# Expert outputs of a mixture-of-experts decoder: from gathers in the combine step to scatters as each tile is done

## The chip, the cores and the metric

The kernel runs on 1 core of one Trainium2 chip, in one launch. The metric is the time of the whole kernel on the device, in microseconds (us), as the median of several runs. TensorE is called PE here, VectorE DVE, ScalarE ACT, GpSimd POOL and SyncE SP.

## The reference: two decoder layers, each ending in experts

8192 tokens (128 sequences of 64) of 128 numbers pass through six sublayers, and a layer norm without weights stands behind each. Two of them are mixtures of experts: one with two experts for each token, one with a single expert. In short:

```
x = norm(x + self_attention(x))
x = norm(x + cross_attention(x, ctx))
x = norm(x + moe2(x))        # 8 experts, top 2, softmax of the two scores as gates
x = norm(x + memory(x))      # a recurrence over 64 steps
x = norm(x + gelu_mixer(x, ctx))
x = norm(x + moe1(x))        # 8 experts, top 1, its probability as gate

moe2: scores = x @ Wg.T; top 2; gates = softmax(the two scores)
      y_e = (silu(x @ W1[e].T) * (x @ W2[e].T)) @ W3[e].T
      out = sum over the two experts of gate * y_e
moe1: probs = softmax(x @ Wr + br); gate, e = max, argmax
      out = gate * (relu(x @ W1[e] + b1[e]) @ W2[e] + b2[e])
```

## The kernel before, in words

**Stages.** Each stage is a block of its own, in which five engine programs run beside each other and wait for each other by counting semaphores; all engines meet between blocks. In the order of time: self attention, cross attention, the top-2 experts (`run_experts`, called "the first expert stage" below, its tiles named `ffn_run_*`), the memory (products, recurrence), the mixer, and the top-1 experts ("the second expert stage", same names). The 8192 tokens are 64 tiles of 128 tokens; tile number t of the tokens lies in `x_all[:, t, :]` in SBUF.

**Routing.** `route` on DVE works out, for one half of the token tiles at a time (`HALF` = 32), at which row of a table sorted by expert each token stands (`dest`). POOL then scatters the tokens' rows into that table in DRAM (`tokens_by_expert`, one indirect DMA of 128 rows for each tile and choice). Each half has its own part of the table, with places left empty so that each 128 rows belong to one expert. The first half's scatters (64 in the first expert stage, 32 in the second) are issued on POOL in the last part of the stage before. `route` for the second half is the last work of that stage, so the second half's scatters are issued inside `run_experts`.

**The expert tiles.** `run_experts` goes over 144 (top 2) or 80 (top 1) tiles of 128 rows of the sorted table; `MID` is half of that. SP loads four tiles at a time. For tile i PE transposes it (L1135), ACT copies the transposed tile (L1168) and the weights of its expert (L1169), PE multiplies (L1143), ACT and DVE make the hidden values (L1176 and L1242 for top 2; L1248 and L1181 for top 1), PE multiplies again (L1152), and DVE copies the result out of PSUM (L1258, or L1260 with a bias). `y_copied` counts these copies. Every four tiles SP stores them to `expert_outputs` in DRAM (L1066), in the order of the sorted table. The first half of the loop is a loop in the code; from `MID` on DVE, SP and POOL have it written out.

**The combine.** A group g is four token tiles, so there are 16 groups. POOL gathers, for each token tile and choice, the 128 rows of `expert_outputs` that belong to its tokens (L1115, 8 indirect DMAs for a group in the first expert stage, 4 in the second). DVE multiplies by the gate and adds the residual (L1200), takes the statistics (L1211, L1216, L1221), POOL takes the power -0.5 (`root`, L1099), DVE normalises (L1228) and SP stores (L1059). The first 8 groups need only the first `MID` expert tiles and run beside the second half of the loop; the last 8 need all tiles and run behind the loop. On POOL's queue stand, in this order: the second half's scatters, each held back until `y_copied` has come within five tiles of it (`turn > 4`), then for each group its gathers and, behind the gathers of group g, `root(g - 1)`.

**The empty rows.** The sorted table is filled with zeros once, in self attention: SP issues two DMAs of 64 KB for each of the 64 tiles (L369) and 16 more behind its loop (L401).

Of the kernel before, what the change touches and what calls it, by code (L numbers as in the profile page):

```python
# [15 lines left out]
P = 128  # L16
# [6 lines left out]
LN_EPS = 1e-5  # L23

# [211 lines left out]
def zeros_for(nc, mk, xs):  # L236

    zeros = mk.sb("zeros", [P, D])
    zeros_set, filled = mk.sem("zeros_set"), mk.sem("xs_filled")
    with nc.Block() as block:  # L240

        @block.vector
        def _(dve):
            dve.memset(zeros[:, :], 0.0).then_inc(zeros_set, 1)
    return {"zeros": zeros, "set": zeros_set, "filled": filled, "xs": [half.rearrange("(n p) d -> n p d", p=P) for half in xs]}


def attention(nc, stage, k, x_in, ctx_in, mask_in, w, x_out, fill=None, f=None, xs=None):
# [3 lines left out]
    with ExitStack() as ctx:  # L252
# [91 lines left out]
        def _(sp):  # L344
# [20 lines left out]
            def step(i):  # L365
                t = i
                if t.exists() and fill:
                    for half in fill["xs"]:
                        sp.dma_start(half[t.n], fill["zeros"][:, :]).then_inc(fill["filled"], 16)  # L369
# [9 lines left out]
                if t.exists():  # L379
                    sp.wait_ge(y_normed, t.count())  # L380
                    dst = f.x_all[:, bass.ds(t.n, 1), :].rearrange("p a d -> p (a d)") if f else out_v[t.n]
                    sp.dma_start(dst, y[:, t.slot(Y), :]).then_inc(stored[t.slot(Y)], 16)
# [15 lines left out]
            if fill:  # L398
                for n in range(NT, Sorted2.ALL // 2):
                    for half in fill["xs"]:  # L400
                        sp.dma_start(half[n], fill["zeros"][:, :]).then_inc(fill["filled"], 16)  # L401
            for n in range(Y):
                sp.wait_ge(stored[n], 16 * NT // Y)

        @block.gpsimd
        def _(pool):
# [36 lines left out]
            else:  # L443
                f.tables(pool)

                def late(i):
                    step(i)
                    if i.c == middle:
# [3 lines left out]
                        pool.wait_ge(f.filled, 16 * Sorted2.ALL)  # L452
                    if i.c < middle + HALF:
                        f.scatter(pool, xs, i.c - middle)
                half_way(pool, step, 4, 4, Tile, middle, late=late, peeled=8)
                for t in range(NT + 4 - middle, HALF):
                    f.scatter(pool, xs, t)
# [344 lines left out]
class Experts:  # L802


    def __init__(self, nc, ctx, stage, a, top2, scattered, gathered):
# [16 lines left out]
        self.x_all = sb("x_all", [P, NT, D])  # L822
        self.dest = sb("dest", [P, K, NT], U32)
        self.source = sb("source", [P, K, NT], U32)
# [20 lines left out]
        self.source_f = sb("source_f", [P, K, HALF])  # L845
# [8 lines left out]
        self.scattered, self.gathered = scattered, gathered  # L854
# [5 lines left out]
    def tables(self, pool):  # L860
# [9 lines left out]
        pool.wait_ge(self.made, 5)  # L870
# [3 lines left out]
    def count_tokens(self, pe, counts, h):  # L874

        pe.wait_ge(self.made, 6)
# [12 lines left out]
    def scatter(self, pool, xs, t):  # L889

        for r in range(self.K):
            self.scatter_one(pool, xs, t, r)

    def scatter_one(self, pool, xs, t, r):

        pool.indirect_dma_start(xs[t // HALF], bass.IndirectOffsetOnAxis(ap=self.dest[:, r, t:t + 1], axis=0), self.x_all[:, t, :], None)\  # L896
            .then_inc(self.scattered, 16)

    def route(self, dve, counts, h):
# [23 lines left out]
        dve.wait_ge(self.made, 6)  # L923
# [49 lines left out]
        link(ts(self.source_f[:, :, :], self.dest_f[:, :, :], float(h * (T // 2 * P)), None, ALU.add))  # L973
        dve.tensor_copy(self.source[:, :, mine], self.source_f[:, :, :])
# [6 lines left out]
        if self.top2:  # L981
# [3 lines left out]
            link(tt(self.gate[:, 1, mine], small["e2"][:, :], self.gate[:, 0, mine], ALU.mult))  # L985


def run_experts(nc, f, k, xs, ys, x_out):
# [3 lines left out]
    MID = kind.ALL // 2  # L992
    w_up, w_down, b_up, b_down, expert_of, x_all, gate = f.w_up, f.w_down, f.b_up, f.b_down, f.expert_of, f.x_all, f.gate
# [21 lines left out]
    with ExitStack() as ctx:  # L1015
        mk = Maker(nc, ctx, stage + "_run")
        sb, ps, sem = mk.sb, mk.ps, mk.sem
        x = sb("x", [P, 2, 4, D])
        y = sb("y", [P, 2, 4, D])
# [6 lines left out]
        r1 = sb("r1", [P, 4, D])  # L1026
        r = sb("r", [P, 2, 4, D])
        stats = sb("stats", [P, 2, 4, 6])
        mv = sb("mv", [P, 2, 4, 2])
        ve = sb("ve", [P, 2, 4])  # L1030
        rstd = sb("rstd", [P, 2, 4])
# [1098 lines left out]
```

## Time and profile before

| What | Value |
|---|---|
| Time of the kernel, median of 3 runs | 2066.25 us (2063.7 to 2067.76) |
| Span of the profiled execution, first to last instruction | 2131.4 us |
| First expert stage: first to last copy out of PSUM | 794.8 to 1060.3 us of the span |
| From there to the next stage's first DMA | 1060.6 to 1168.3 us |
| Second expert stage: first to last copy out of PSUM | 1882.7 to 2065.1 us |
| From there to the end | 2065.4 to 2131.4 us |
| PE, DVE, ACT, POOL busy over the span | 64%, 66%, 52%, 47% |

The profiled execution has no time of its own beside its span: the span is what the trace gives, and it is 65 us longer than the median of the runs without a profile. All durations below are from the profiled execution.

### The profile page before, as it was taken

The numbers are of one execution on the slowest core, as the hardware profiler recorded it, in microseconds if no ns is written. First come the engines' busy times: TensorE is split into PE (matmuls) and PEld (weight loads), VectorE is DVE, ScalarE is ACT, GpSimd is POOL, SyncE is SP. The second block draws the span as 40 slices with busy tenths as digits, with TensorE's granted clock in tenths as the row PEclk, the third lists the DMA queues.
The fourth block names the chain that finished last, engine by engine and source line by source line (L and its number), as shares of the span: only waits on it lengthen the run. The fifth ranks groups of instructions, "written<-read, shape, count | busy, mean of one in ns | idle before, by whom it ended". The sixth has DMA issues, their size and how long they took to land. (4 is left out here: it accounts for less than half of the span.)

```text
span 2131.4 us, 61164 instructions
## 1 busy us (share of the span) xinstructions
PE 1357.8 (64%) x18328; PEld 1105.5 (52%) x18383; DVE 1406.7 (66%) x4922; ACT 1101.9 (52%) x3264; POOL 994.8 (47%) x1543
## 2 busy tenths in 40 slices
PE   6999984799978738788700899400001786679850
PEld 4777762677756527787700577300000665479750
DVE  4999982688776643346634566499997677644565
ACT  4777762577746525555500455365555565456430
POOL 3666661455558855435475344111112455842345
PEclk9999995999989959999955899755555998889985
DMA  1222221311112113334322244300000422222232
GB/s 39 76 74 74 74 65 47 102 50 54 45 47 68 58 49 104 102 91 123 109 64 58 69 100 100 53 1 1 1 1 16 144 74 64 71 84 78 78 88 70
DMA packets 218918, 141.81 MB, mean 67 GB/s; under 512 B 22380, under 2 KB 207254, under 8 KB 218646
## 3 DMA queue, kind: packets, MB, share of 16 engines
q1 hardware_dynamic: 206486, 114.94, 20.1%
q0 software_dynamic: 12288, 25.19, 3.8%
q8 instruction: 61, 1.00, 0.2%
q14 instruction: 83, 0.68, 0.1%
HBM read 75.92 MB, written 55.67 MB: 62 GB/s over the span
## 5 line engine op out<-in xcount | busy, mean ns | idle before, releaser
L1143 PE MATMUL ffn_run_up_ps<-ffn_run_xt,ffn_run_w_now 128*128 128x128 f32 x1792 | 251.5, 285 | 72.0 <-ACT ffn_run_w_now L1169 39.2
L1143 PEld LDWEIGHTS ffn_run_up_ps<-ffn_run_xt,ffn_run_w_now 128*128 128x128 f32 x1792 | 225.5, 197 | 87.1 <-ACT ffn_run_xt L1168 59.3
L896 POOL DMA_INDIRECT tokens_by_expert<-ffn_x_all,ffn_dest x192 | 192.1, 1001 | 137.6 <-DVE ffn_run_y L1258 47.2
L1115 POOL DMA_INDIRECT ffn_run_yg<-expert_outputs,ffn_source x192 | 185.0, 963 | 142.0 <-issue 59.7
L1862 PE MATMUL mixer_m_ps<-mixer_mine,mem_state_coef 128*64 128x64 f32 x4 | 0.5, 334 | 283.7 <-DVE mixer_off_in L2003 283.7
L1152 PE MATMUL ffn_run_y_ps<-ffn_weights,ffn_run_h 128*128 x1216 | 175.2, 278 | 0.8 <-DVE ffn_run_y L1258 0.4
L1152 PEld LDWEIGHTS ffn_run_y_ps<-ffn_weights,ffn_run_h 128*128 128x128 f32 x1216 | 156.8, 195 | 1.1 <-issue 1.1
L1242 DVE TENSOR_TENSOR ffn_run_h<-ffn_run_up_ps,ffn_run_act 128x256 f32<-128x256 f32 x144 | 60.6, 421 | 144.0 <-ACT ffn_run_act L1176 121.1
L1588 POOL TENSOR_TENSOR recur_rho<-recur_var_eps_new,k_half 128x1 f32<-128x1 f32 x64 | 34.7, 543 | 248.1 <-DVE recur_var_eps_new L1682 248.1
L1862 PEld LDWEIGHTS mixer_m_ps<-mixer_mine,mem_state_coef 128*64 128x64 f32 x4 | 0.3, 204 | 283.8 <-DVE mixer_ones L2001 283.8
L1169 ACT COPY ffn_run_w_now<-ffn_weights 128x512 f32 x224 | 140.3, 626 | 0.0
L429 POOL TENSOR_TENSOR self_k_ex<-self_kt,k_head_mask 128x256 f32<-128x256 f32 x128 | 75.8, 613 | 120.0 <-ACT self_kt L646 120.0
L429 POOL TENSOR_TENSOR cross_k_ex<-cross_kt,k_head_mask 128x256 f32<-128x256 f32 x128 | 75.9, 614 | 110.4 <-ACT cross_kt L646 110.0
L1841 POOL TENSOR_TENSOR mixer_rstd<-mixer_ve,k_half 128x1 f32<-128x1 f32 x128 | 69.1, 553 | 84.0 <-DVE mixer_ve L2029 83.7
L1168 ACT COPY ffn_run_xt<-ffn_run_xt_ps 128x128 f32<-128x128 f32 x224 | 58.4, 261 | 92.8 <-PE ffn_run_xt_ps L1135 67.4
L714 DVE TENSOR_REDUCE cross_top<-cross_s_ps_ps 128x16 f32<-128x1024 f32 x64 | 77.9, 1217 | 26.4 <-PE cross_s_ps_ps L519 19.1
L1248 DVE TENSOR_TENSOR ffn_run_sums<-ffn_run_up_ps,ffn_weights 128x512 f32<-128x512 f32 x80 | 55.1, 688 | 58.9 <-PE ffn_run_up_ps L1143 37.3
L1200 DVE SCALAR_TENSOR_TENSOR ffn_run_r<-ffn_run_yg,ffn_gate,ffn_x_all 128x128 f32<-128x128 f32 x128 | 43.6, 340 | 76.0 <-DMA ffn_run_yg<-expert_outputs,ffn_source 72.9
L1176 ACT ACTIVATE ffn_run_act<-ffn_run_up_ps 128x256 f32<-128x256 f32 x144 | 55.5, 386 | 72.2 <-PE ffn_run_up_ps L1143 61.4
L714 DVE TENSOR_REDUCE self_top<-self_s_ps_ps 128x16 f32<-128x1024 f32 x64 | 77.8, 1215 | 14.7 <-PE self_s_ps_ps L523 14.7
L1181 ACT ACTIVATE ffn_run_h<-ffn_run_sums 128x512 f32<-128x512 f32 x80 | 50.4, 630 | 70.0 <-DVE ffn_run_sums L1248 65.6
L1135 PE MATMUL ffn_run_xt_ps<-k_ident,ffn_run_x 128*128 128x128 f32 x224 | 62.3, 280 | 33.9 <-DMA ffn_run_x<-tokens_by_expert 33.9
(367 smaller groups left out, 4830.2 us busy)
## 6 DMA issues: line engine op xcount, KB each, us to landing
ffn_run_x<-tokens_by_expert SPq DMA_DIRECT2D x56, 256.0 KB
expert_outputs<-ffn_run_y SPq DMA_DIRECT2D x56, 256.0 KB
tokens_by_expert<-fill_zeros SPq DMA_DIRECT2D x144, 64.0 KB, 1.6
memory_rows<-products_row SPq DMA_DIRECT2D x16, 390.0 KB, 4.7
ffn_weights<-memory_rows SPq DMA_DIRECT2D x16, 390.0 KB
self_x<-in_x SPq DMA_DIRECT2D x64, 64.0 KB, 1.9
self_xr<-in_x SPq DMA_DIRECT2D x64, 64.0 KB, 1.9
x<-self_y SPq DMA_DIRECT2D x64, 64.0 KB, 1.5
```

Of the source, the lines that this page charges most:

```text
L429: pool.tensor_tensor(k_ex[:, t.slot(2), b, :, :], kt[:, t.slot(2), b * S:(b + 1) * S].unsqueeze(1).to_broadcast([P, 4, S]), k["head_mask4" ...
L714: dve.tensor_reduce(top[:, t.slot(2), :].rearrange("p (q h) -> p q h", q=4), s_ps, AX, ALU.max).then_inc(top_ready, 1)
L896: pool.indirect_dma_start(xs[t // HALF], bass.IndirectOffsetOnAxis(ap=self.dest[:, r, t:t + 1], axis=0), self.x_all[:, t, :], None)\
L1115: pool.indirect_dma_start(yg[:, g % 4, n, m, :], None, rows, bass.IndirectOffsetOnAxis(ap=f.source[:, m, 4 * g + n:4 * g + n + 1], axis=0))\
L1135: nc.tensor.transpose(xt_ps[t.slot(2)][:, 0:P], x[:, slot, t.c % 4, :], k["ident"][:, :]).then_inc(x_turned, 1)
L1143: mm = nc.tensor.matmul(up_ps[t.slot(2)][:, c * P:(c + 1) * P], w_now[:, t.slot(2), c * P:(c + 1) * P], xt[:, t.slot(2), :], start=True, s ...
L1152: mm = nc.tensor.matmul(y_ps[t.slot(2)][:, 0:D], h[:, t.slot(4), c, :], w_down[:, bass.ds(e_now, 1), c, :], start=(c == 0), stop=(c == FC ...
L1168: act.copy(xt[:, t.slot(2), :], xt_ps[t.slot(2)][:, 0:P]).then_inc(x_copied, 1)
L1169: act.copy(w_now[:, t.slot(2), :], w_up[:, bass.ds(e_ahead, 1), :].rearrange("p a n -> p (a n)")).then_inc(w_taken, 1)
L1176: act.activation(act1[:, t.slot(2), :], up_ps[t.slot(2)][:, 0:HID], ACT.Silu).then_inc(silu_ready, 1)
L1242: dve.tensor_tensor(h[:, t.slot(4), :, :].rearrange("p c n -> p (c n)"), up_ps[s2][:, HID:2 * HID], act1[:, s2, :], ALU.mult)\
L1841: pool.tensor_tensor(rstd[n][:, s2, :], ve[n][:, s2, :], k["half"][:, 0:1], ALU.pow).then_inc(rstd_ready[n], 1)
```

## The change

Each row of the sorted table is now 130 numbers wide: the token's 128, the number of the row its result is to go to (1 + 2 * token + choice, or 1 + token), and, for top 2, its gate. `x_all` has the two extra columns. POOL sets the row number with an iota, adds one before the second choice is scattered (`relabelled`), and copies the gates of the choice into place. Scatters go choice by choice, no longer tile by tile, and are no longer held back by `y_copied`. DVE reads number and gate back from each loaded tile (`ids`, `gates`; a row that was left empty has the number 0 and is sent to a spare row of its own), multiplies by the gate as it copies the result out of PSUM, and puts the result into `y_all`, which holds all tiles. POOL scatters each tile from there to `expert_outputs`, which is now in the order of the tokens. The combine reads four token tiles with one plain DMA on SP (`fetch`). DVE adds (two additions of 128x512 for a group for top 2, four multiply-and-adds for top 1) and works out `shift` = -mean * rstd; the normalisation is ACT's (`norm`, an activation with scale and bias). Groups 0 to 7 are combined two for every eight tiles from tile `START` on (96 of 144, or 48 of 80). Groups have four buffers where they had two. ACT's second half of the loop is now written out too. The zero fill is 64 larger DMAs for four tables (the second expert stage has its own now), none behind the loop.

```diff
-    def scatter_one(self, pool, xs, t, r):
-        pool.indirect_dma_start(xs[t // HALF], bass.IndirectOffsetOnAxis(ap=self.dest[:, r, t:t + 1], axis=0), self.x_all[:, t, :], None)\
-            .then_inc(self.scattered, 16)
+    def scatter(self, pool, xs, h, n):
+        r, t = n // HALF, h * HALF + n % HALF
+        mine = slice(h * HALF, (h + 1) * HALF)
+        if n == HALF:
+            pool.wait_ge(self.scattered[h], 16 * HALF)
+            pool.tensor_scalar(self.x_all[:, mine, D], self.x_all[:, mine, D], 1.0, None, ALU.add).then_inc(self.relabelled, 1)
+        if self.top2 and n % HALF == 0:
+            pool.wait_ge(self.gated, h + 1)
+            pool.tensor_copy(self.x_all[:, mine, D + 1], self.gate[:, r, mine]).then_inc(self.relabelled, 1)
+            pool.wait_ge(self.relabelled, 3 * h + 1 + 2 * r)
+        pool.indirect_dma_start(xs[h], bass.IndirectOffsetOnAxis(ap=self.dest[:, r, t:t + 1], axis=0), self.x_all[:, t, :], None)\
+            .then_inc(self.scattered[h], 16)
...
         @block.gpsimd
         def _(pool):
-            for t in range(HALF, NT):
-                for m in range(K):
-                    turn = K * (t - HALF) + m
-                    if turn > 4:
-                        pool.wait_ge(y_copied, turn - 4)
-                    f.scatter_one(pool, xs, t, m)
...
-                for n in range(4):
-                    for m in range(K):
-                        turn = K * (4 * g + n) + m
-                        if g < N_G // 2 and turn > 3:
-                            pool.wait_ge(y_copied, MID + turn - 3)
-                        pool.indirect_dma_start(yg[:, g % 4, n, m, :], None, rows,
...
+            for n in range(K * HALF):
+                f.scatter(pool, xs, 1, n)
+            for t in range(kind.ALL):
+                pool.wait_ge(y_copied, t + 1)
+                pool.indirect_dma_start(ys, bass.IndirectOffsetOnAxis(ap=ids[:, t:t + 1], axis=0), y_all[:, t, :], None)\
+                    .then_inc(stored[t // MID], 16)
+                u, part = (t - START) // 8, (t - START) % 8
+                if t >= START and part == 5 and u < 4:
+                    root(2 * u)
+                    root(2 * u + 1)
+            for g in range(N_G // 2, N_G):
+                root(g)
...
         @block.sync
         def _(sp):
+            def fetch(g):
+                if g >= 4:
+                    sp.wait_ge(summed, g - 3)
+                sp.dma_start(yg[:, g % 4, :, :, :], ys_v[g]).then_inc(fetched[g % 4], 16)
...
-                if t.exists() and t.c % 4 == 3:
-                    n, slot, uses = four(t)
-                    sp.wait_ge(y_copied, t.count())
-                    sp.dma_start(ys_v[n], y[:, slot, :, :]).then_inc(stored[slot], 16)
...
+                    if part == 0 and u == 0:
+                        sp.wait_ge(stored[0], 16 * MID)
+                    if part == 0 and u < 4:
+                        fetch(2 * u)
+                        fetch(2 * u + 1)
...
         @block.scalar
+                for n in tiles:
+                    no = act.activation(out[:, s4, n, :], r[:, s4, n, :], ACT.Identity, bias=shift[:, s4, n:n + 1], scale=rstd[:, s4, n:n + 1])
...
         @block.vector
+                if top2:
+                    dve.tensor_tensor(r1[:, :, :], yg[:, s4, :, 0, :], x_all[:, mine, 0:D], ALU.add).then_inc(partly, 1)
+                    dve.wait_ge(partly, g + 1)
+                    dve.tensor_tensor(r[:, s4, :, :], yg[:, s4, :, 1, :], r1[:, :, :], ALU.add).then_inc(summed, 1)
...
-                        dve.tensor_copy(y[:, slot, t.c % 4, :], y_ps[t.slot(2)][:, 0:D]).then_inc(y_copied, 1)
+                        dve.tensor_scalar(mine, y_ps[t.slot(2)][:, 0:D], gates[:, slot, t.c % 4:t.c % 4 + 1], None, ALU.mult).then_inc(y_copied, 1)
...
+                if i.static and START <= i.c < kind.ALL:
+                    u, part = (i.c - START) // 8, (i.c - START) % 8
+                    if u < 4 and part in (0, 2):
+                        add(2 * u + part // 2)
+                    elif u < 4 and part in (1, 3):
+                        spread(2 * u + part // 2)
+                    elif u < 4 and part == 4:
+                        moments(2 * u)
+                        moments(2 * u + 1)
+                    if 1 <= u < 5 and part == 3:
+                        shifts(2 * u - 2)
+                        shifts(2 * u - 1)
```

POOL's queue in the first expert stage, before: the 64 scatters of the second half, the gathers (`ffn_run_yg`) of groups 0 and 1, and then 8 gathers and a `root` (`ffn_run_rstd`) in turn.

```order
L896 DMA tokens_by_expert<-ffn_x_all,ffn_dest 9216x128 x64
L1115 DMA ffn_run_yg<-expert_outputs,ffn_source 128x128 x16
L1099 TENSOR_TENSOR ffn_run_rstd<-ffn_run_ve,k_half 128x4
L1115 DMA ffn_run_yg<-expert_outputs,ffn_source 128x128 x8
L1099 TENSOR_TENSOR ffn_run_rstd<-ffn_run_ve,k_half 128x4
```

The same queue of the changed kernel, from the start of the stage.

```order
L1125 IOTA ffn_run_spare 128x144
L1127 TENSOR_SCALAR ffn_run_spare<-ffn_run_spare 128x144
L903 COPY ffn_x_all<-ffn_gate 128x32
L905 DMA tokens_by_expert<-ffn_x_all,ffn_dest 9216x130 x32
L900 TENSOR_SCALAR ffn_x_all<-ffn_x_all 128x32
L903 COPY ffn_x_all<-ffn_gate 128x32
L905 DMA tokens_by_expert<-ffn_x_all,ffn_dest 9216x130 x32
L1132 DMA expert_outputs<-ffn_run_y_all,ffn_run_ids 34817x128 x102
L1123 TENSOR_TENSOR ffn_run_rstd<-ffn_run_ve,k_half 128x4 x2
L1132 DMA expert_outputs<-ffn_run_y_all,ffn_run_ids 34817x128 x8
```

No gather is left; 144 scatters of results stand behind the 64 of tokens, and the first two roots stand behind the scatter of tile 101.

DVE's program in the first expert stage, before, where a group is combined beside the loop: two steps of the loop, each with a quarter of group 0.

```order
L1242 TENSOR_TENSOR ffn_run_h<-ffn_run_up_ps,ffn_run_act 128x256
L1258 COPY ffn_run_y<-ffn_run_y_ps 128x128
L1200 SCALAR_TENSOR_TENSOR ffn_run_r<-ffn_run_yg,ffn_gate,ffn_x_all 128x128
L1200 SCALAR_TENSOR_TENSOR ffn_run_r<-ffn_run_yg,ffn_gate,ffn_run_r 128x128
L1211 BN_STATS ffn_run_stats<-ffn_run_r 128x6
```

The changed kernel, steps 98 to 100 of the loop (the second group of a pair, then the moments of both).

```order
L1290 TENSOR_TENSOR ffn_run_h<-ffn_run_up_ps,ffn_run_act 128x256
L1307 TENSOR_SCALAR ffn_run_y_all<-ffn_run_y_ps,ffn_run_gates 128x128
L1235 TENSOR_TENSOR ffn_run_r<-ffn_run_yg,ffn_x_all 128x512
L1237 TENSOR_TENSOR ffn_run_r<-ffn_run_yg,ffn_run_r 128x512
L1290 TENSOR_TENSOR ffn_run_h<-ffn_run_up_ps,ffn_run_act 128x256
L1307 TENSOR_SCALAR ffn_run_y_all<-ffn_run_y_ps,ffn_run_gates 128x128
L1251 BN_STATS ffn_run_stats<-ffn_run_r 128x6 x4
L1290 TENSOR_TENSOR ffn_run_h<-ffn_run_up_ps,ffn_run_act 128x256
L1307 TENSOR_SCALAR ffn_run_y_all<-ffn_run_y_ps,ffn_run_gates 128x128
L1258 BN_AGGR ffn_run_mv<-ffn_run_stats 128x2 x4
L1263 TENSOR_SCALAR ffn_run_ve<-ffn_run_mv 128x4
```

A quarter of a group for each step has become the whole addition in one step, the whole statistics in the next, and the moments of two groups in a third; the normalisation is gone from DVE.

## Rows read from the trace of the kernel before

**Rows 1.** Busy time by stage: stretch, length, then each engine's busy us.
```profile
783.60:1061.00 277.40, 227.42 (x1872) 216.29 (x1872) 128.66 (x456) 158.87 (x433) 131.43 (x136) 0.97 0.36 104
1061.00:1168.20 107.20, 0.00 (x0) 0.00 (x0) 42.85 (x169) 0.00 (x0) 70.19 (x72) 0.51 0.23 64
1872.00:2065.40 193.40, 163.65 (x1360) 158.82 (x1360) 102.80 (x293) 104.90 (x240) 69.80 (x72) 0.96 0.29 83
2065.40:2131.40 66.00, 0.00 (x0) 0.00 (x0) 32.33 (x140) 0.00 (x0) 39.38 (x40) 0.51 0.26 76
```

**Rows 2.** POOL's groups behind the first loop: count, busy us, mean ns, idle.
```profile
L1115 POOL DMA_INDIRECT ffn_run_yg<-expert_outputs,ffn_source x64 | 61.8, 966 | 22.8 <-issue 22.8
L1099 POOL TENSOR_TENSOR ffn_run_rstd<-ffn_run_ve,k_half 128x4 f32<-128x4 f32 x8 | 8.4, 1050 | 8.6 <-DVE ffn_run_ve L1221 8.5
```

**Rows 3.** Timeline, both ends of the two stretches behind the loops.
```profile
1060.33 0.29 DVE L1258 COPY ffn_run_y<-ffn_run_y_ps 128x128 f32<-128x128 f32 x1
...
1161.25 1.62 SPq L1059 DMA_DIRECT2D x<-ffn_run_out  x2
...
2065.05 0.29 DVE L1260 TENSOR_TENSOR ffn_run_y<-ffn_run_y_ps,ffn_weights 128x128 f32<-128x128 f32 x1 [0.20 <-PE ffn_run_y_ps L1152]
...
2113.72 0.95 POOL L1115 DMA_INDIRECT ffn_run_yg<-expert_outputs,ffn_source  x1 [0.30 <-issue]
...
2116.27 0.35 DVE L1200 SCALAR_TENSOR_TENSOR ffn_run_r<-ffn_run_yg,ffn_gate,ffn_x_all 128x128 f32<-128x128 f32 x1 [1.76 <-DMA ffn_run_yg<-expert_outputs,ffn_source]
...
2120.48 1.62 SPq L1059 DMA_DIRECT2D decoded<-ffn_run_out  x2
```

**Rows 4.** Copies out of PSUM by stretch: length, DVE busy (count).
```profile
794.50:906.50 112.00, 16.55 (x59) 1.00 0.33 99
908.50:928.50 20.00, 3.65 (x13) 1.00 0.36 100
973.00:1060.70 87.70, 14.05 (x50) 1.00 0.41 114
...
1984.00:2065.40 81.40, 9.03 (x32) 0.94 0.30 84
```

**Rows 5.** DVE's groups, 973 to 1061 us.
```profile
L1242 DVE TENSOR_TENSOR ffn_run_h<-ffn_run_up_ps,ffn_run_act 128x256 f32<-128x256 f32 x48 | 20.0, 417 | 22.2 <-ACT ffn_run_act L1176 13.9 <-issue 6.5 <-PE ffn_run_y_ps L1152 1.8
```

**Rows 6.** DVE's groups, 1984 to 2065.4 us.
```profile
L1248 DVE TENSOR_TENSOR ffn_run_sums<-ffn_run_up_ps,ffn_weights 128x512 f32<-128x512 f32 x30 | 20.5, 683 | 3.6 <-PE ffn_run_up_ps L1143 3.5
L1200 DVE SCALAR_TENSOR_TENSOR ffn_run_r<-ffn_run_yg,ffn_gate,ffn_x_all 128x128 f32<-128x128 f32 x32 | 10.9, 339 | 10.8 <-DMA ffn_run_yg<-expert_outputs,ffn_source 10.8
L1211 DVE BATCH_NORM_STATS2 ffn_run_stats<-ffn_run_r 128x6 f32<-128x128 f32 x32 | 9.4, 295 | 1.1
L1260 DVE TENSOR_TENSOR ffn_run_y<-ffn_run_y_ps,ffn_weights 128x128 f32<-128x128 f32 x32 | 9.0, 282 | 1.4 <-PE ffn_run_y_ps L1152 1.4
L1228 DVE TENSOR_SCALAR ffn_run_out<-ffn_run_r,ffn_run_mv,ffn_run_rstd 128x128 f32<-128x128 f32 x29 | 8.6, 363 | 10.4 <-POOL ffn_run_rstd L1099 10.4
L1216 DVE BATCH_NORM_AGGREGATE ffn_run_mv<-ffn_run_stats 128x2 f32<-128x6 f32 x32 | 3.0, 156 | 0.0
L1221 DVE TENSOR_SCALAR ffn_run_ve<-ffn_run_mv 128x4 f32<-128x4 f32 x8 | 1.4, 170 | 0.3
```

**Rows 7.** POOL's timeline, start of the first expert stage.
```profile
784.33 0.97 POOL L896 DMA_INDIRECT tokens_by_expert<-ffn_x_all,ffn_dest  x1 [12.06 <-POOLq L154]
785.60 0.97 POOL L896 DMA_INDIRECT tokens_by_expert<-ffn_x_all,ffn_dest  x1 [0.30 <-issue]
```

**Rows 8.** DMAs by line: KB of one, median us from issue to landing.
```profile
products_x<-x SPq DMA_DIRECT2D x16, 256.0 KB, 3.0
ffn_weights<-in_L_ffn_b SPq DMA_DIRECT2D x1, 512.0 KB, 5.0
```

**Rows 9.** An ACT activation with a bias for each partition: min/median/max ns.
```profile
L649 ACT ACTIVATE cross_qt<-cross_front_ps,cross_b_cols x64: 358/359/380, 353.5 to 726.5; 128x128 f32<-128x128 f32 x64
```

**Rows 10.** SP's timeline, end of self attention.
```profile
321.35 7.55 SPq L401 DMA_DIRECT2D tokens_by_expert<-fill_zeros  x16
332.68 0.34 SPq L347 DMA_DIRECT2D cross_w_t<-in_L_xattn_Wq  x1
```

More of the change, by code:

```diff
@@ L802, with __init__ @@
 class Experts:
-    def __init__(self, nc, ctx, stage, a, top2, scattered, gathered):
+    def __init__(self, nc, ctx, stage, a, top2, scattered, stored):
         self.nc, self.stage, self.a, self.top2 = nc, stage, a, top2
@@ L874, in count_tokens @@
     def count_tokens(self, pe, counts, h):
-        pe.wait_ge(self.made, 6)
+        pe.wait_ge(self.made, 7)
         pe.wait_ge(self.selected, h + 1)
@@ L1076, in _ @@
-            sp.wait_ge(f.scattered, 16 * K * HALF)
-            half_way(sp, step, 8, 1, kind, MID - 8, second)
-            for g in range(PER * (MID // 8 - 2), N_G):
+                if i.static and i.c >= START - 4:
+                    u, part = (i.c - START + 4) // 8, (i.c - START + 4) % 8
+                    if part == 0 and u == 0:
[3 more added lines that the diff above has]
+                        fetch(2 * u + 1)
+                    if part == 6 and u >= 2:
+                        keep(2 * u - 4)
+                        keep(2 * u - 3)
@@ new lines, in _ @@
+            sp.wait_ge(f.scattered[0], 16 * K * HALF)
+            half_way(sp, step, 8, 0, kind, MID - 8, second)
+            sp.wait_ge(stored[1], 16 * MID)
+            first = [2 * u - 4 + n for u in range(2, 6) if START - 4 + 8 * u + 6 >= kind.ALL for n in range(2)]
+            for g in range(N_G // 2, N_G):
+                fetch(g)
+                if first:
+                    keep(first.pop(0))
+                if g >= N_G // 2 + 3:
+                    keep(g - 3)
+            for g in range(N_G - 3, N_G):
@@ L1122, in _ @@
+            for g in range(N_G // 2, N_G):
+                root(g)
         @block.tensor
@@ L1266, in _ @@
+            dve.wait_ge(numbered, 2)
             half_way(dve, step, 3, 0, kind, MID)
+            if START + 32 + 3 >= kind.ALL:
+                shifts(N_G // 2 - 2)
+                shifts(N_G // 2 - 1)
             for g in range(N_G // 2, N_G):
-                for part in range(5):
-                    combine(g, part, 4 * (g + 1))
+                add(g)
+                spread(g)
+                moments(g)
                 if g > N_G // 2:
-                    combine(g - 1, 6)
-                    combine(g - 1, 7)
```

284 lines of the change are left out of this document (145 added, 139 removed).

## The prediction, made before the changed kernel had run

> **What bounds the kernel now.** I read the busy time by stage first. In the two stretches behind the expert loops, 107.2 and 66.0 us long, PE and ACT do nothing at all and DVE is busy less than half the time; POOL is busy for 70.2 and 39.4 us [rows 1]. The groups of POOL say with what: 64 gathers of 966 ns each and 8 roots [rows 2]. Two indirect DMAs that wait for nothing start 1.27 us apart [rows 7], so 64 of them take 81 us whatever the data. The timeline gives the length to be compared: from the last copy out of PSUM (1060.33) to the end of the last store's issue (1162.87) 102.5 us, and in the second stage from 2065.05 to 2122.10, 57.0 us [rows 3]. These two stretches are bound by POOL's issue of gathers.
>
> Inside the loops I counted copies by stretch. In the first stage they come every 1.90 us while POOL scatters tokens (59 in 112 us), every 1.54 us where no indirect DMA runs (13 in 20 us), and every 1.75 us beside the combine (50 in 87.7 us) [rows 4]. So PE could go at 1.54, and something in the company of POOL's DMAs costs up to 0.36 us for each tile. In the second stage the combine's half takes 2.54 us for a tile (32 in 81.4 us) [rows 4], and DVE's groups there show why: 10.8 us of waiting for gathered rows and 10.4 us for roots, which stand behind gathers on POOL [rows 6].
>
> **The change part by part.**
>
> *Behind the first loop.* No gather is left. After the last copy (0.29 us) comes one scatter, whose rows can be used 2.55 us after its issue if I take the last gather's case (2113.72 to 2116.27) [rows 3]; no row shows the landing of a scatter. Then a fetch of 512 KB, 5.0 us by a load of the same size [rows 8]. Together 7.8 us. The eight groups are then DVE's: two additions of 128x512 at 0.683 (the same form from PSUM), four statistics at 0.295, four aggregates at 0.156, and two small operations at 0.170 [rows 6] make 3.5 us, with waits for its own results 3.6; eight groups 28.8 us. Behind the last group one root, 1.05 us [rows 2], the shift, four normalisations at 0.36 us [rows 9], hops and the store's issue: 3.5 us. Sum 40.1 instead of 102.5: **62 us less**. The transfers should hide: 512 KB read for a group at 5.0 us alone is more than DVE's 3.6, but four fetches are issued ahead. Were they not to overlap at all, eight would take 40 us and the gain would be 51.
>
> *Behind the second loop.* A fetch of 256 KB is 3.0 us [rows 8]: 5.8 us to the first group. A group is four multiply-and-adds at 0.339 and the rest as above, 3.5 us; eight are 28, and 3.5 behind. Sum 37.3 instead of 57.0: **20 us less**.
>
> *The second loop.* For eight tiles with two groups DVE has 8 x (0.683 + 0.282) = 7.7, adds 2.7, statistics 2.4, aggregates 1.2, four small operations 0.7, the row numbers 0.7, and some ten waits for its own results, 1.5: 17 us or 2.1 for a tile [rows 6]. The normalisation's 0.363 us for each of 32 tiles [rows 6] is ACT's now. Over 32 tiles 67 us instead of 81.4: **14 us less**. POOL isn't late here: 32 token scatters are 41 us, and 1.27 for a tile is less than 2.1.
>
> *The first loop.* POOL has 64 + 144 scatters of 1.27 us. It starts at 784.3 [rows 7]; 1.2 us for the row numbers, 81.3 for 64 scatters, and 2.6 for the drain before the second choice is relabelled: 869.4. Scatter of tile t ends at 869.4 + 1.27 (t + 1), so POOL is about 40 tiles behind and gains on the loop. Tile 101 is done at 999, the two roots behind it at 1001. DVE waits for them in step 107. Tile 96 is copied at about 977 now; from there eight tiles with two groups are 8 x (0.417 + 0.34) for the two operations of a tile [rows 5], 2.7 for additions, 2.4 + 1.2 + 0.7, row numbers and gates 1.0, own waits 1.8: 15.9 us, 2.0 a tile. Step 107 comes at 999: the roots are just late, by 2 us. SP's wait for the first 72 results (869.4 + 91.4 + 2.6 = 963) lies before its step at 970 and holds nothing; behind it are the next loads of tiles. ACT's two normalisations in four steps of eight add 0.36 each, which fits in 2.0. End of the loop: 977 + 32 x 2.0 + 16 x 1.75 = 1069, with the wait 1071, where it is 1060 now: **11 us more**.
>
> *The same loop without a profile.* The span is 65 us above the median of the runs. If part of that is the 0.36 us a tile in the first 60 tiles, the loop before is up to 22 us shorter in the runs that are timed, but the changed one isn't, since POOL's 1001 us doesn't move: DVE and PE just wait for it. Bounds 0 and 25 us; I take the middle, since nothing in the trace says how much: **12 us more**.
>
> *The rest.* The 16 fills behind self attention's loop take 7.55 us of SP, and the next stage begins 3.8 us after them [rows 10]; the last stores need some 1.5 us of that anyway, and a block that clears semaphores is new: **4.5 us less**. Fills inside the loop shrink from two DMAs a tile to one, SP having room. In cross attention POOL's relabelling comes some 3 us after the scatter it waits for, so it costs only its own two small operations; with those, a longer memset and more semaphores to clear I put **1.5 us more**. Wider rows (520 bytes for 512) have no row; I take them as equal, and up to 2 us a stage as the other end.
>
> *Sum:* 62 + 20 + 14 + 4.5 - 11 - 12 - 1.5 = 76 us of the span, from 2131 to 2055. The runs stand to the span as 2066 to 2131, so 74 us off the median: **1993 us**.
>
> **A rule against it.** Through the stretch behind the first loop POOL's indirect DMAs run beside DVE's operations between SBUF buffers and keep a mean of 966 ns [rows 2], against 970 ns for the first two of the stage with DVE idle [rows 7]. The Trainium skill, page "SBUF — State Buffer", section "SBUF: two separate sides", says that while DVE runs a two-port operation GpSimd is locked out and cannot write its descriptors. By that rule every scatter would be later by an operation's length; by the trace it adds nothing.
>
> **Rivals.**
> 1. *Scatters of results cost more than those of tokens* (slower). With a price c for each of 208 scatters the first stage's POOL ends at 784 + 13 + 208 c. At c = 1.27 that is 1061, inside the loop. Each scatter that waited for one DVE operation of 0.34 us would make c 1.61 and POOL's end 1132: 61 us lost, gain 13 of the span, about 2053. The gain is gone at c = 1.68; at 1.9 POOL ends at 1192 and the kernel takes about 2110. That is the mechanism of the page's rule. Against it: 966 and 970 ns. Chance 8% for slower, 2% within 0.2%.
> 2. *The combine in lumps holds the loops back.* One step takes two additions of 128x512, the next four statistics, a third both groups' moments, and ACT's two normalisations follow. PE's buffers allow about two tiles of slack. If these steps don't average out, 2.5 us a tile for the 32 tiles of each stage: 16 + 13 us more, about 2021; with serial fetches behind the loop 2031. For it: own waits in each lump. Chance 16%.
> 3. *The loops lose their other stalls too.* SP's stores of four tiles are gone, and DVE doesn't wait for gathers in the loop. If the first loop ends as it does now (1060) and nothing of the 12 us comes, 23 us better: about 1971. POOL's end at 1061 allows no more. Chance 14%.
> 4. *My forecast*, 60%, with its own range 1975 to 2012.
>
> **How the numbers follow.** Range: down to rival 3 with some room, 1958; up to rival 2 with serial fetches, 2033. Faster by over 0.2% (4 us, about what a measurement of this kernel can tell from no change): 0.90, same 0.02, slower 0.08.
>
> **What the changed profile would show.** Behind the loops: no POOL DMA but the last, DVE busy with few gaps, 40 and 37 us to the last store. POOL in the first stage: 208 indirect DMAs 1.27 us apart to about tile 110, then waiting for copies. Copies every 1.9 us up to tile 96, then 2.0; a wait of DVE for a root near 1000 us. The forecast is wrong if POOL's pitch isn't 1.27, if copies with the combine come at 2.5 us, if fetches leave DVE idle between groups, or if the loop's pace in the first 72 tiles changes.

## The result, and the profile after

The changed kernel takes **2002.16 us** (median of 4 runs, 2000.04 to 2004.25) where the kernel before takes 2066.89: a ratio of 0.9688, 95% interval 0.9674 to 0.9701, or 65 us less. The forecast was 1993 us with a range of 1958 to 2033.

The trace that stands ahead of the prediction is of an execution 65 us longer than the timed runs. So the kernel before was run again (b_again, below): that execution has a span of 2063.6 us, the changed kernel's has 1998.3, and these two are compared here.

Busy time by stage, first of the kernel before in b_again (stretch, length, busy us of PE, weight loads, DVE, ACT and POOL, then granted clock, DMA share, GB/s). The rows are cross attention, the first loop, what is behind it, memory and mixer, the second loop, what is behind it.

```profile
331.20:769.00 437.80, 325.29 (x6393) 255.22 (x6393) 300.62 (x623) 247.06 (x656) 257.04 (x390) 0.90 0.20 58
769.00:1000.40 231.40, 219.47 (x1872) 212.00 (x1872) 126.90 (x455) 165.48 (x433) 131.74 (x136) 0.98 0.43 125
1000.40:1105.20 104.80, 0.00 (x0) 0.00 (x0) 43.40 (x170) 0.00 (x0) 69.95 (x72) 0.51 0.24 65
1105.20:1809.30 704.10, 346.07 (x2668) 251.70 (x2668) 533.01 (x2723) 369.22 (x1418) 234.46 (x488) 0.75 0.21 53
1809.30:1997.60 188.30, 164.61 (x1360) 160.23 (x1360) 103.10 (x293) 104.89 (x240) 69.78 (x72) 0.94 0.30 86
1997.60:2063.60 66.00, 0.00 (x0) 0.00 (x0) 32.33 (x140) 0.00 (x0) 39.35 (x40) 0.51 0.27 76
```

The same of the changed kernel:

```profile
326.60:764.50 437.90, 327.01 (x6393) 255.68 (x6393) 299.86 (x619) 246.77 (x656) 258.62 (x395) 0.90 0.20 58
764.50:1038.40 273.90, 227.00 (x1872) 217.37 (x1872) 129.87 (x492) 176.12 (x465) 209.67 (x219) 0.92 0.36 108
1038.40:1080.50 42.10, 0.00 (x0) 0.00 (x0) 22.72 (x96) 13.07 (x32) 11.76 (x10) 0.52 0.51 155
1080.50:1787.30 706.80, 348.31 (x2668) 253.40 (x2668) 531.08 (x2719) 370.11 (x1418) 235.78 (x490) 0.75 0.22 53
1787.30:1955.50 168.20, 159.50 (x1360) 155.25 (x1360) 100.25 (x310) 114.01 (x263) 115.08 (x119) 0.97 0.33 94
1955.50:1998.30 42.80, 0.00 (x0) 0.00 (x0) 20.90 (x114) 16.67 (x42) 11.90 (x12) 0.53 0.44 126
```

Row by row the 65.3 us between the two spans come apart, with 331.2 less 326.6 for self attention:

| Stretch | Forecast | Measured |
|---|---|---|
| Self attention and its boundary | -4.5 | -4.6 |
| Cross attention | +1.5 | +0.1 |
| First loop | +23 (11 and 12) | **+42.5** |
| Behind the first loop | -62 | -62.7 |
| Memory and mixer | 0 | +2.7 |
| Second loop | -14 | -20.1 |
| Behind the second loop | -20 | -23.2 |
| Sum | -76 | -65.3 |

The +2.7 of memory and mixer wasn't traced to a cause. The first loop is the row to look at. It was PE's: busy for 219.5 of 231.4 us. Now it is 42.5 us longer with the same matmuls, while POOL's busy time went from 131.7 to 209.7. POOL's groups in it (count, busy us, mean ns, idle before and its releasers):

```profile
L1132 POOL DMA_INDIRECT expert_outputs<-ffn_run_y_all,ffn_run_ids x144 | 140.1, 973 | 43.7 <-issue 33.8 <-DVE ffn_run_y_all L1307 9.9
L905 POOL DMA_INDIRECT tokens_by_expert<-ffn_x_all,ffn_dest x64 | 61.5, 961 | 19.5 <-issue 18.9 <-POOL ffn_x_all L903 0.6
L1123 POOL TENSOR_TENSOR ffn_run_rstd<-ffn_run_ve,k_half 128x4 f32<-128x4 f32 x8 | 8.5, 1068 | 0.1
```

Busy and idle of these three rows are 273.4 us; with 3 us for row numbers and gates that is all of the time from the stage's start (764.5) to the end of the last scatter (1040.8). 208 indirect DMAs take 264.8 of it, 1.27 us each, and none of the result scatters waited for a copy longer than 0.5 us. What DVE does meanwhile, in its timeline (start, duration, operation, idle time before and its releaser):

```profile
924.59 0.34 DVE L1307 TENSOR_SCALAR ffn_run_y_all<-ffn_run_y_ps,ffn_run_gates 128x128 f32<-128x128 f32 x1
944.83 0.69 DVE L1235 TENSOR_TENSOR ffn_run_r<-ffn_run_yg,ffn_x_all 128x512 f32<-128x512 f32 x1 [19.89 <-DMA ffn_run_yg<-expert_outputs]
...
979.56 0.16 DVE L1269 SCALAR_TENSOR_TENSOR ffn_run_shift<-ffn_run_mv,ffn_run_rstd 128x4 f32<-128x4 f32 x1 [13.75 <-POOL ffn_run_rstd L1123]
```

DVE reaches tile 96 at 924.6 and waits 19.9 us for the first fetch, which waits for POOL's scatter of tile 71 (it ends at 939.4, SP issues the fetch at 940.7); then 13.7 us for the first root, which stands behind the scatter of tile 101. Both waits are for POOL.

Behind the first loop, where [rows 3] had 102.5 us between the last copy and the end of the last store's issue:

```profile
1039.84 0.96 POOL L1132 DMA_INDIRECT expert_outputs<-ffn_run_y_all,ffn_run_ids  x1 [0.30 <-issue]
...
1046.08 0.69 DVE L1235 TENSOR_TENSOR ffn_run_r<-ffn_run_yg,ffn_x_all 128x512 f32<-128x512 f32 x1 [7.68 <-DMA ffn_run_yg<-expert_outputs]
...
1048.98 0.69 DVE L1235 TENSOR_TENSOR ffn_run_r<-ffn_run_yg,ffn_x_all 128x512 f32<-128x512 f32 x1
...
1065.80 7.96 SPq L1082 DMA_DIRECT2D x<-ffn_run_out  x4
```

The last scatter can be used 2.2 us after its issue (SP's fetches start at 1042.08), the first group's rows are there at 1046.08, and a group takes 2.90 us from one addition to the next. From the last copy (1038.05) to 1073.76 it is 35.7 us.

### The profile page after: what moved, and what is told of

The parts are those of the page before. It is cut to its first block and busy times, and to the rows that moved or that the text cites. A ratio compares the mean times of both kernels' runs of the same rounds, so it can differ in the third digit from the quotient of the medians.

```text
span 1998.3 us, 61159 instructions
## 1 busy us (share of the span) xinstructions
PE 1350.8 (68%) x18382; PEld 1097.1 (55%) x18383; DVE 1371.0 (69%) x4870; ACT 1158.3 (58%) x3392; POOL 1034.6 (52%) x1587
## 5 line engine op out<-in xcount | busy, mean ns | idle before, releaser
L1162 PE MATMUL ffn_run_up_ps<-ffn_run_xt,ffn_run_w_now 128*128 128x128 f32 x1792 | 249.8, 284 | 47.6 <-DVE ffn_run_h L1290 20.3
L1132 POOL DMA_INDIRECT expert_outputs<-ffn_run_y_all,ffn_run_ids x224 | 218.4, 975 | 87.5 <-issue 46.4
L718 DVE TENSOR_REDUCE self_top<-self_s_ps_ps 128x16 f32<-128x1024 f32 x64 | 77.7, 1214 | 14.7 <-PE self_s_ps_ps L527 14.7
L1187 ACT ACTIVATE ffn_run_out<-ffn_run_r,ffn_run_shift,ffn_run_rstd 128x128 f32<-128x128 f32 x128 | 53.4, 483 | 57.6 <-DVE ffn_run_shift L1269 57.6
L1447 POOL TENSOR_TENSOR products_rr<-products_mse,k_half 128x1 f32<-128x1 f32 x64 | 34.6, 541 | 95.8 <-DVE products_mse L1600 87.4
L644 ACT COPY self_prob_t<-self_pt_ps_ps 128x512 f32<-128x512 f32 x128 | 68.9, 589 | 20.7 <-PE self_pt_ps_ps L562 20.7
```

What stands on the lines that cost most here:

```text
L644: act.copy(prob_t[:, 4 * h:4 * h + 4, :], pt_ps[h][:, :, :]).then_inc(pt_copied, 1)
L718: dve.tensor_reduce(top[:, t.slot(2), :].rearrange("p (q h) -> p q h", q=4), s_ps, AX, ALU.max).then_inc(top_ready, 1)
L1132: pool.indirect_dma_start(ys, bass.IndirectOffsetOnAxis(ap=ids[:, t:t + 1], axis=0), y_all[:, t, :], None)\
L1162: mm = nc.tensor.matmul(up_ps[t.slot(2)][:, c * P:(c + 1) * P], w_now[:, t.slot(2), c * P:(c + 1) * P], xt[:, t.slot(2), :], start=True, s ...
```

## Experiments

Every ratio is to the kernel before, in the runs of the same chip; the changed kernel's is 0.9688.

**b_again: the kernel before, once more, with a profile.**

> The kernel before, unchanged, for a second profile. If its span was long because of the recording itself, the span is near 2131 us again and copies of the first stage come every 1.9 us. If that one execution was disturbed, the span is near 2066 us, and the 65 us are missing in places that can be read: I look at the first stage's copies (1.9 or 1.55 us a tile), cross attention (435 or 423 us) and the two stretches behind the loops.

It took 2065.44 us (one run), its trace spans 2063.6. Copies out of PSUM by stretch (length, DVE busy and count, clock, DMA share, GB/s), of b_again and then of the changed kernel:

```profile
779.50:891.50 112.00, 20.16 (x72) 1.00 0.38 115
```

```profile
775.30:887.30 112.00, 24.63 (x72) 1.00 0.33 95
```

72 copies in 112 us in both, where [rows 4] had 59. The pace of 1.90 us was that execution's and not the kernel's; so was the 1.75 us beside the combine (b_again has the last 72 copies in 109.0 us, 1.51 each), and so was 13 us of cross attention (450.9 there, 437.8 here), and in all the first loop was 45.6 us longer there (277.0 for 231.4, by the same cut). What slowed that one execution isn't shown: the single operations took as long there as in b_again (a matmul of L1143 279 and 278 ns), the gaps between them were longer.

**b_nohold: the wait of token scatters left out.**

```diff
-                    if turn > 4:
-                        pool.wait_ge(y_copied, turn - 4)
```

> The kernel before without the wait that holds each token scatter back until the copies have come within five tiles. Theory A, POOL's indirect DMAs in company slow the loop by 0.36 us a tile: the 64 scatters are over after 81 us, some 45 tiles, and 15 tiles go faster, 5 us less in all. Theory B, the wait itself slows the loop (POOL waking on each copy): copies come every 1.55 us from the first tile on, about 20 us less. Theory C, neither does, and the pace of 1.9 was that execution's: no change within 4 us.

2066.4 us, ratio 0.9999 (0.9984 to 1.0015). That is theory C: the 5 us of theory A and the 20 of theory B lie outside the interval, so neither POOL's DMAs in company nor the hold slow the loop by such amounts.

**b_nohold2: the wait of the first eight groups' gathers left out.**

```diff
-                        if g < N_G // 2 and turn > 3:
-                            pool.wait_ge(y_copied, MID + turn - 3)
```

> The kernel before without the wait that holds the gathers of the first eight groups back to one for each copy. In the second stage's combine half DVE waited 10.5 us for gathered rows and 10.4 us for roots. If this hold is what makes the rows late, both go and the kernel is about 20 us faster. If the rows are late because gathers stand on POOL's queue behind a root that waits up to 14.7 us for DVE's variance, nothing changes (within 3 us).

Ratio 1.001 (0.9995 to 1.0025): the hold costs nothing. What does cost time is seen on POOL's timeline in b_again's second stage:

```profile
1911.02 0.94 POOL L1115 DMA_INDIRECT ffn_run_yg<-expert_outputs,ffn_source  x1 [0.30 <-issue]
1926.68 1.05 POOL L1099 TENSOR_TENSOR ffn_run_rstd<-ffn_run_ve,k_half 128x4 f32<-128x4 f32 x1 [14.71 <-DVE ffn_run_ve L1221]
1927.92 1.00 POOL L1115 DMA_INDIRECT ffn_run_yg<-expert_outputs,ffn_source  x1 [0.19 <-issue]
```

The next gathers stand behind a root that waits 14.7 us for DVE, and DVE then waits for them, 10.5 us in all by its groups there, and 10.4 us for roots:

```profile
L1200 DVE SCALAR_TENSOR_TENSOR ffn_run_r<-ffn_run_yg,ffn_gate,ffn_x_all 128x128 f32<-128x128 f32 x32 | 10.9, 339 | 10.5 <-DMA ffn_run_yg<-expert_outputs,ffn_source 10.5
...
L1228 DVE TENSOR_SCALAR ffn_run_out<-ffn_run_r,ffn_run_mv,ffn_run_rstd 128x128 f32<-128x128 f32 x30 | 8.8, 362 | 10.4 <-POOL ffn_run_rstd L1099 10.4
```

In the changed kernel's second loop DVE waits for neither in that half, only for PE. 20.9 us of waits went, the loop is 20.1 us shorter. That the one makes the other is read from the two traces; no run took these waits out alone.

**a_extra: more scatters for POOL.**

```diff
+                if t < (24 if top2 else 12):
+                    pool.indirect_dma_start(other, bass.IndirectOffsetOnAxis(ap=ids[:, t:t + 1], axis=0), y_all[:, t, :], None)\
+                        .then_inc(stored[0], 16)
```

> The changed kernel with more work for POOL: the results of the first 24 tiles of the first expert stage, and of the first 12 of the second, are scattered a second time, into a table that nothing reads. In the changed kernel's trace POOL issues in the first stage without a pause to 1040.8 us; in the second it waits for copies. If POOL's issue bounds the first stage, it ends 24 x 1.27 = 30 us later and the second stays as it is (12 x 1.27 = 15 us fit in its waits): 30 us slower, about 2032 us. If the first stage were bound by its loop's lumps and POOL only kept up, less than 10 us slower. If POOL bounds the second too, 45.

2037.53 us, ratio 0.9867 (0.9837 to 0.9897). The two loops of its trace:

```profile
767.40:1071.90 304.50, 229.18 (x1872) 219.54 (x1872) 130.56 (x492) 176.26 (x465) 233.01 (x243) 0.87 0.34 102
...
1819.80:1993.70 173.90, 161.08 (x1360) 156.44 (x1360) 100.39 (x310) 114.01 (x263) 126.40 (x131) 0.96 0.33 96
```

The first is 30.6 us longer for 24 scatters, 1.27 each: POOL's issue is the first loop's length. The second, where I expected nothing, is 5.7 longer: with 15 us more POOL is late there too, for the fetches at the start of its combine, for which DVE waits 4.3 us. So the span is 36.5 us longer than the changed kernel's (2034.8 for 1998.3) and not 30.

**a_start108: the first stage's combine from tile 108.**

```diff
-    START = MID + (24 if top2 else 8)
+    START = MID + (36 if top2 else 8)
```

> The changed kernel with the combine of the first stage started at tile 108 instead of 96. There DVE waited 19.9 us for the first fetch and 13.7 us for the first root. If POOL's 208 indirect DMAs and 8 roots bound the stage (they fill it from its start to 1040.8 us), both waits cost nothing: the same time within 3 us. If the waits cost what they last, 20 to 30 us faster.

2001.35 us, ratio 0.9692 (0.9673 to 0.9711): the same. Its loop and what is behind it:

```profile
762.50:1033.30 270.80, 227.01 (x1872) 215.96 (x1872) 130.28 (x491) 173.00 (x457) 207.16 (x218) 0.93 0.36 107
1033.30:1078.00 44.70, 0.00 (x0) 0.00 (x0) 22.80 (x99) 16.25 (x40) 13.63 (x12) 0.54 0.52 159
```

DVE's waits didn't go, they moved: 3.8 us for fetches and 29.7 for roots in the loop, 33.5 together, where the changed kernel has 20.3 and 14.6, 34.9 together. They are where DVE sits out what POOL is late by, at whatever place it meets POOL. POOL's last scatter ends 275.1 us behind the stage's start (1037.6 less 762.5) where it was 276.3; the last copy comes 3.1 us earlier, and the stretch behind it is 2.6 longer.

**a_pair: one root for two groups.**

```diff
+            def roots(u):
...
+                pool.tensor_tensor(rstd[:, s4:s4 + 2, :], ve[:, s4:s4 + 2, :], k["half"][:, :].unsqueeze(1).to_broadcast([P, 2, 4]), ALU.pow)\
+                    .then_inc(rstd_ready, 2)
```

> The changed kernel with one root for the two groups of a pair (four POOL operations on 128x8 instead of eight on 128x4 beside the loop, in each expert stage). If POOL bounds the first stage, each root left out takes 1.0 us off its end: 4 us faster, none of it in the second stage. If the loop's own pace bounds it, no change.

2001.97 us, ratio 0.9686 (0.9664 to 0.9708). The form of the expectation held, its size didn't: a root on 128x8 takes 1.67 us, two on 128x4 2.08, so four pairs save 1.6 us and not 4, too little for these runs to show.

```profile
L1130 POOL TENSOR_TENSOR ffn_run_rstd<-ffn_run_ve,k_half x8: 1667/1674/2014, 980.3 to 1956.9; 128x8 f32<-128x8 f32 x8
```

**a_dvenorm: the normalisation on DVE.**

```diff
-                    no = act.activation(out[:, s4, n, :], r[:, s4, n, :], ACT.Identity, bias=shift[:, s4, n:n + 1], scale=rstd[:, s4, n:n + 1])
+                    no = dve.tensor_scalar(out[:, s4, n, :], r[:, s4, n, :], rstd[:, s4, n:n + 1], shift[:, s4, n:n + 1], ALU.mult, ALU.add)
```

> The changed kernel with the normalisation on DVE again (one operation with scale and shift for each token tile, as it stands in ACT's program now, at the same places). By my account DVE has 0.36 us more for each of 128 tiles. Behind each loop DVE is what the time is made of: 8 x 1.45 = 11.6 us more in each, 23 in all. In the first loop POOL bounds and nothing is added. In the second, DVE has 17 us of waiting for PE in 85 us: if that takes it up, nothing more, 2025 us in all; if lumps can't be taken up, up to 11.6 more, 2037 us. If ACT's part had been worth nothing, no change.

2009.43 us, ratio 0.973 (0.970 to 0.976). Its four stretches:

```profile
764.30:1036.00 271.70, 226.86 (x1872) 217.68 (x1872) 137.92 (x524) 166.26 (x433) 208.12 (x218) 0.91 0.37 108
1036.00:1085.60 49.60, 0.00 (x0) 0.00 (x0) 31.26 (x129) 0.00 (x0) 11.33 (x11) 0.52 0.45 132
1790.80:1958.00 167.20, 157.81 (x1360) 154.26 (x1360) 105.12 (x333) 105.42 (x240) 115.36 (x119) 0.98 0.33 95
1958.00:2007.80 49.80, 0.00 (x0) 0.00 (x0) 32.34 (x156) 0.00 (x0) 11.38 (x12) 0.51 0.38 108
```

No loop is longer (271.7 for 273.9, 167.2 for 168.2), each stretch behind one is 7 us longer (49.6 for 42.1, 49.8 for 42.8). ACT's part is worth some 7 us behind each loop and nothing in them. I had 11.6 for each and so 2025 us in all: four such operations in a row take 1.12 us and not 4 x 0.36, which makes 9.0; the rest of the difference isn't traced.

**a_pooladd: an addition of each group behind the first loop on POOL.**

```diff
+            def first_add(g):
+                pool.wait_ge(fetched[g % 4], (g // 4 + 1) * 16)
+                pool.wait_ge(summed, g - 1)
+                pool.tensor_tensor(r1[:, g % 2, :, :], yg[:, g % 4, :, 0, :], x_all[:, 4 * g:4 * g + 4, 0:D], ALU.add).then_inc(partly, 1)
```

> The changed kernel with the first of the two additions of 128x512 of each group behind the first loop given to POOL, which only has a root for each group there. A group is 2.92 us of DVE now, 0.72 of it this addition. If POOL's addition (some 1.2 us by its 128x256 multiplication of 0.61) runs beside DVE at no cost to it, 8 x 0.72 = 5.8 us less: 1996 us. If operations of POOL and DVE between SBUF buffers hold each other up, the gain is gone, or it is some microseconds slower.

2002.2 us, ratio 0.9693 (0.9665 to 0.9722): nothing. The profiled execution was the slowest of the four (2010.62 us, the others 2001.0 to 2002.4), so its lengths are not compared, only what waited for what. The first two groups came 2.2 us apart. Later DVE waited twice, 3.0 and 2.8 us, for an addition of POOL that itself waited for a fetch:

```profile
1063.17 1.18 POOL L1141 TENSOR_TENSOR ffn_run_r<-ffn_run_yg,ffn_x_all 128x512 f32<-128x512 f32 x1 [2.44 <-DMA ffn_run_yg<-expert_outputs]
...
1064.48 0.69 DVE L1248 TENSOR_TENSOR ffn_run_r<-ffn_run_yg,ffn_run_r 128x512 f32<-128x512 f32 x1 [3.04 <-POOL ffn_run_r L1141]
```

SP's queue shows why the fetches were late:

```profile
1058.55 0.38 SPq L1082 DMA_DIRECT2D x<-ffn_run_out  x1
1058.97 0.51 SPq L1078 DMA_DIRECT2D ffn_run_yg<-expert_outputs  x1
1060.89 0.38 SPq L1082 DMA_DIRECT2D x<-ffn_run_out  x1
1061.31 0.51 SPq L1078 DMA_DIRECT2D ffn_run_yg<-expert_outputs  x1
```

Each fetch stands behind the store of a group four earlier, whose normalisation it doesn't need.

**a_fetch** puts these fetches two groups ahead; **a_best** adds POOL's addition and the start at tile 108.

```diff
-                if g >= N_G // 2 + 3:
-                    keep(g - 3)
-            for g in range(N_G - 3, N_G):
+                if g >= N_G // 2 + 5:
+                    keep(g - 5)
+            for g in range(N_G - 5, N_G):
```

> The changed kernel with another order on SP behind the loops: the fetches of groups 12 to 15 stand two groups ahead of where they stood, no longer behind the store of a group whose buffer they don't need. In the changed kernel DVE waited only 0.2 us for those fetches, so alone this is worth nothing: the same within 3 us.

> Together: the first addition of each group behind the first loop on POOL, the earlier fetches, and the combine of the first stage from tile 108 on. With POOL's addition alone the groups came 2.2 to 2.9 us apart until DVE and POOL waited for fetches that stood behind stores on SP. If that order was what ate the gain, groups come every 2.3 us, 8 x 0.65 = 5 us less behind the loop, and up to 3 us less in the loop: 1994 us. If the transfers themselves (512 KB of fetch and 256 KB of store for each group) are the limit at some 2.9 us a group, nothing is gained behind the loop, and it takes 1999 to 2002 us.

1998.13 us, ratio 0.9671 (0.9656 to 0.9686), and 1999.33 us, 0.9674 (0.9659 to 0.969). The first isn't told from the changed kernel (the intervals overlap; the stretch behind its first loop is 41.5 us for 42.1). In the second the groups came 2.2 and 2.9 us apart in turn, 2.5 on average and not 2.3, and from the third group on neither DVE nor POOL waited for a fetch. So neither the order on SP nor the transfers set that pace. The last section shows what lengthens every second group.

**a_again and a_pf: the changed kernel, and the version without the later start.**

> The changed kernel, unchanged, on the same chip as the next one, to compare the two directly: 2002 us if the runs so far are typical of it, within 3 us.

> The changed kernel with POOL's addition and the earlier fetches, and with the combine from tile 96 on as in the changed kernel. With the start at tile 108 the loop was 2.7 us shorter and the rest 3 us longer, since the last pair's normalisation and stores fell behind the loop, beside the fetches that everything waits for. If that is so, the stretch behind the loop is now 39 us instead of 42.5 and the kernel 3 to 5 us faster than the changed one. If the transfers set the pace there, it is the same.

On one chip 2001.41 us (0.9687, 0.9667 to 0.9707) and **1993.15 us** (0.9655, 0.9631 to 0.9679), five runs each, means 2000.0 and 1993.6. The ratios' intervals overlap a little, so 6 to 8 us is likely and not certain; what the trace shows of it is 2.9 us, behind the first loop:

```profile
1037.80:1077.00 39.20, 0.00 (x0) 0.00 (x0) 19.22 (x89) 13.07 (x32) 21.66 (x18) 0.54 0.55 166
```

The spans of the two profiled versions (1998.3 and 1992.3) differ by 6.0 us; the other 3.1 lie in stretches that this edit leaves alone, 1.8 of them in memory and mixer. Where they come from stays open.

## Why the prediction was right, and where it was off

The whole came out nearer than its parts. The first loop came out 19.5 us worse than forecast and memory and mixer 2.7; all other rows together came out 11.5 better. That these errors cancel in part is luck: 76 us were forecast by the spans and 65 measured. By the prediction's own sign ("if the loop's pace in the first 72 tiles changes") its view of the first loop was wrong: the copies came every 1.55 us and not every 1.90.

*The bound before.* Right. In b_again too POOL issues 64 gathers without a pause behind the first loop, and groups come 11.1 us apart. This is read from traces; no run of the kernel before had gathers taken away.

*Behind the loops, -62 and -20.* Right, as POOL's gathers gone and DVE's work left. Measured on the same cut as the prediction's 40.1, 35.7: the group is 2.90 us and not 3.6, because operations that don't wait for each other overlap (four statistics 0.87 and not 4 x 0.295, four aggregates 0.38 and not 0.62). The stretch before was shorter as well in b_again, so the difference held. In the second stage a group is 2.57 us and not 3.5, while the first one's rows come after 8.2 us and not 5.8; what is left of both is some 3 us more than forecast.

*The second loop, -14.* The mechanism was right (the waits for gathers and roots go), the size short by 6 us. The prediction had the roots stand behind gathers; b_again shows the other half too, gathers behind roots that wait for DVE. I took 2.1 us a tile from a sum of DVE's durations; it is 1.94 (42 copies in 81.4 us). PE is busy for 79.1 of these 81.4 us, so this is PE's own pace, with the combine beside it. The copies in that stretch (length, DVE busy and count, clock, DMA share, GB/s):

```profile
1874.10:1955.50 81.40, 12.09 (x42) 1.00 0.36 104
```

*The first loop, +11 and +12, measured +42.5.* This is the term that was mis-sized, and the step is: "something in the company of POOL's DMAs costs up to 0.36 us for each tile", with "Bounds 0 and 25 us" for what a run without a profile would change. The company costs the loop nothing that these runs can tell: b_again goes at 72 copies in 112 us beside scatters, the changed kernel does so beside scatters back to back, and b_nohold changes nothing. The 0.36 us was that one execution's. The loop before is 45.6 us shorter than in the trace I read (231.4 for 277.0), while the changed one is only 13.8 shorter than forecast (273.9 for 277.0 + 10.7 = 287.7), since POOL holds it: 10.7 + 45.6 - 13.8 = 42.5. So the term put at 12, the middle of its bounds 0 and 25, measured 31.8, outside them. POOL's end itself was exact: put 276.7 us behind the stage's start (1061 less 784.3), it came at 276.3. The 2 us that I had DVE wait at tile 107, and the nothing for the first fetch, became 13.7 and 19.9 for the same reason: up to tile 96 the copies come every 1.55 us, and so run further ahead of POOL. POOL caught up with the copies only at the last tiles, where I had it do so at tile 110.

*The scale.* "The runs stand to the span as 2066 to 2131" spread the 65 us over the whole kernel, which took 2 us off the gain. They lay in places: of the 67.8 us between the spans of the two traces 45.6 lay in the first loop, 13 in cross attention, 5 in the second loop, 2 behind the first.

*Rival 1* fell by its size: a scatter of results takes 973 ns on average, one of tokens 961, and the 24 extra ones 1.27 us each. Its mechanism is there, though. By the rule of the Trainium skill, page "SBUF — State Buffer", section "SBUF: two separate sides", POOL would wait out DVE's two-port operations, and the trace agrees for the few scatters that meet one: five of 144 took 1.28 to 1.40 us (last section), 1.9 us in all. So "by the trace it adds nothing" went too far: 966 ns is the mean of gathers and 970 that of the first two scatters of a stage, and a mean hides a few held ones. By the rival's own sums the gain at c = 1.61 would be 76 - 61 = 15 us of the span and not 13. *Rival 2* fell in the second loop (1.94 us a tile with lumps); in the first POOL hides it. *Rival 3* had the right observation, that POOL's end allows no more than -23, and lost because that end stayed while the loop before was shorter.

## What to carry to other kernels

Count the issues on the queue with a fixed price (208 x 1.27 us here) and compare them with the loop's time in an undisturbed execution: a span that is 3% over the median of the runs is a reason not to read a loop's pace from that trace. A work item moved from behind a loop into it is free only up to the slack of its engine, and past that every microsecond comes back: 62.7 us were won behind the first loop and 42.5 paid in it. After a bound engine is relieved, read the next queue in program order; with POOL's addition alone nothing was gained, and with SP's fetches put ahead of the stores as well the stretch behind the loop was 2.9 us shorter.

## What was not expected of the hardware

POOL and DVE hold each other up, but only where the one begins at certain moments of the other, and POOL's indirect DMAs are no exception. In the changed kernel's first loop (start and duration in us):

```profile
948.45 0.68 DVE L1235 TENSOR_TENSOR ffn_run_r<-ffn_run_yg,ffn_x_all 128x512 f32<-128x512 f32 x1
```

```profile
947.37 0.96 POOL L1132 DMA_INDIRECT expert_outputs<-ffn_run_y_all,ffn_run_ids  x1 [0.30 <-issue]
948.64 1.32 POOL L1132 DMA_INDIRECT expert_outputs<-ffn_run_y_all,ffn_run_ids  x1 [0.30 <-DVE ffn_run_y_all L1307]
```

Five of the 144 result scatters took 1.28 to 1.40 us instead of 0.96. Each began 0.18 to 0.24 us after a DVE addition of 128x512 (two operands in SBUF) had begun, with 0.45 to 0.50 us of it left. One that began with 0.20 left took 1.03, and three that began 0.05 to 0.64 us before an addition kept 0.96. In the traces of a_extra, a_start108, a_pair, a_dvenorm, a_fetch, a_best, a_again and a_pf, too, every scatter of the first loop over 1.1 us (34 in all) began inside such an addition. The delays are 1.9 us of 276 in the changed kernel, since such additions are few; a kernel with many beside its indirect DMAs would have to count them.

Behind the first loop of a_pf the same shows on arithmetic:

```profile
1050.72 1.16 POOL L1141 TENSOR_TENSOR ffn_run_r<-ffn_run_yg,ffn_x_all 128x512 f32<-128x512 f32 x1
```

```profile
1051.19 0.73 DVE L1274 TENSOR_SCALAR ffn_run_ve<-ffn_run_mv 128x4 f32<-128x4 f32 x1
```

DVE's small operation on 128x4 takes 0.17 us five times of eight and 0.70 to 0.73 three times; these three began inside an addition of POOL and ended with it, to within 0.04 us. In these three groups that is 0.55 us each, most of what sets the groups of 2.9 us apart from those of 2.2. A root is held as well: in the changed kernel, where POOL has only the roots there, four roots that began 0.09 to 0.15 us into a DVE addition took 1.44 to 1.47 us, and three that began 0.07 to 0.16 us before one took 1.01. This agrees with the same section of the Trainium skill, which gives the shared port to whichever begins first, for the whole operation, and blocks the other. Not all of it does: the three additions that began within a root kept their 0.69 us.
